# Deformable convolution: hats of three taps in one VectorE instruction, and a second group of values copied by VectorE

## The chip, the core and the metric

The kernel runs on one core of a Trainium2 chip. The metric is the device time of one execution in microseconds (us), the median of several runs. A core has four engines that compute, each with its own instruction queue, worked off in order: TensorE (PE in the profile, with PEld for its weight loads), VectorE (DVE), ScalarE (ACT) and GpSimd (POOL). SyncE (SP) issues most DMAs. Engines wait for each other by semaphores.

## The reference, cut to what matters

The input is two images of 64 channels, 128 x 128 pixels, fp32. A small encoder and decoder of 3x3 convolutions is added to it, then a deformable 3x3 convolution is added to that. The change lies in the second:

```python
x = x + _L0_conv_ref(_gn(x), ...)             # encoder, decoder: not touched
x = x + _L1_conv_ref(_gn(x), w_off, b_off, w_def)

offsets = _conv2d(x, w_off, b_off, 1, 1)      # dy, dx for each of 9 taps and each pixel
py = hs + iy + dy                             # where tap k reads, a fraction of a pixel
px = ws + ix + dx
val = gather(y0, x0, (1 - wy) * (1 - wx)) + ...   # bilinear, four neighbours
out = einsum('bckhw,ock->bohw', val, w_def)
```

## The kernel before

Up to about 755 us the kernel computes the first part and the offsets. From there to the end (1282.5 us) it computes the deformable convolution in 32 strips of four output rows, both images at once. A bilinear gather is written as a matrix product: for a window of pixels and a tap, the weight of a pixel is hat(y distance) x hat(x distance), with hat(d) = 1 - min(|d|, 1). For each strip and each of the nine taps (UNITS = 9):

- TensorE makes the distances of a tap in one of two PSUM slots (`distances`, L1039, eight matmuls).
- ScalarE takes their absolute value into the SBUF tile `dist` (`absolute`, L1460, 128x1024: both images, and y and x side by side). `dist` holds six taps (DIST_RING).
- VectorE clamps it in place, min(d, 1) - 1 (`hats`, L1850, 128x1024), and multiplies the y half by the x half into the tile `hat` (`product`, L1860, 128x512). `hat` is double, one half for each of two strips.

When the nine taps of a strip are in `hat`, TensorE multiplies windows of pixels by them in six groups (`sample_group`, L1086): groups 0 to 3 of three blocks, groups 4 and 5 of two, with a few narrow matmuls of the edges behind group 5 (L1098). Even groups use PSUM banks 4 and 5, odd ones banks 6 and 7. A group's values are copied to the SBUF tile `val`: group 2 by VectorE (L511), the others by ScalarE (L1463), where group 5 has two small edge copies behind it. Then TensorE multiplies `val` by the weights in four parts (`weigh`, L1160 and L1155, banks 6 and 7), and VectorE adds the residual (`strip_result`, L1886, output `outt`).

The order on each engine is written out by hand. In step s TensorE runs, for n = 0 to 8, `distances(s + 1, n)`, then the parts of `weigh(s - 1)` at n = 1, 2, 3 and 4, then the groups of strip s: group 0 at n = 5, groups 1 and 2 at n = 6, group 3 at n = 7, groups 4 and 5 at n = 8. So one step of TensorE reads

d0 d1 W01 d2 W23 d3 W45 d4 W678 d5 G0 d6 G1 G2 d7 G3 d8 G4 G5 edges

with d the distances of the next strip, W the weighing of the last one by taps and G the groups of this one. These short names are used below. W01 waits until all six groups of the last strip are copied. G1 waits for the result of the last strip (its banks hold the sum), G2 and later ones for the copy of the group two ahead, and dn for the absolute value of tap n - 2. ScalarE runs the absolute value of tap n, then the copies of the groups of that n. VectorE runs, for each n, the hats of tap n and the product of tap n - 1; the result of the last strip stands ahead of the hats at n = 5 (RESULT_AT), and the copy of group 2 behind the product at n = 6.

Of the kernel before, what the change touches and what calls it, by code (L numbers as in the profile page):

```python
# [10 lines left out]
ALU = mybir.AluOpType  # L11
# [69 lines left out]
DIST_RING = 6  # L81
# [4 lines left out]
ACT_GROUPS = [0, 1, 3, 4, 5]  # L86
DVE_GROUPS = [2]
# [3 lines left out]
RESULT_AT = 5  # L91
# [81 lines left out]
def build(nc, x, w4, w3, wds, wdec, woff, boff, wdef, wtaps, gmat, ident, sel, rampc, selg, places, out):  # L173
    es = ExitStack()
    with es:
# [103 lines left out]
        dist = in_stage("dist", [P, DIST_RING, 2, BANK])  # L279
# [241 lines left out]
        def dist_at(j, n):  # L521

            return dist[:, (UNITS * j + n) % DIST_RING]

# [278 lines left out]
        def _(pe):  # L803
# [252 lines left out]
            def sample_group(s, j, count, g):  # L1056

                if g == 0:
                    pe.wait_ge(win_in[j], count)
                    pe.wait_ge(prod_dve, UNITS * (s + 1))  # L1060
                    settled(pe)
# [186 lines left out]
        def _(act):  # L1248
# [200 lines left out]
            def absolute(s, j, n, first=False):  # L1449
                act.wait_ge(dist_made, UNITS * s + (n + 1))  # L1450

                if n >= DIST_RING or not first:
                    m_ = n - DIST_RING
                    q = s if m_ >= 0 else s - 1
                    m_ %= UNITS
                    act.wait_ge(prod_dve, UNITS * q + (m_ + 1))
                elif n == DIST_RING - 1:
                    act.wait_ge(edge_hats, 1)
                slot = 2 * dist_slot(j, n)
                act.activation(dist_at(j, n), psum[:, slot:slot + 2, :], ACT.Abs).then_inc(dist_abs, 1)  # L1460
# [47 lines left out]
            def edge_absolute(e):  # L1508
                act.wait_ge(edge_dist, e + 1)
                if e:  # L1510
                    act.wait_ge(prod_dve, UNITS * STRIPS)
                act.activation(dist[:, DIST_RING - 1, :, 0:K * W0], psum[:, 0:2, 0:K * W0], ACT.Abs).then_inc(edge_abs, 1)

# [26 lines left out]
        def _(dve):  # L1540
# [305 lines left out]
            def hats(s, j, n):  # L1846

                dve.wait_ge(dist_abs, UNITS * s + (n + 1))
                d = dist_at(j, n)
                dve.tensor_scalar(d, d, 1.0, 1.0, ALU.min, ALU.subtract).then_inc(hats_made, 1)  # L1850

            def product(s, j, n):
                if n == 0 and not (isinstance(s, int) and s < 2):
                    dve.wait_ge(vals_made, GROUPS * (s - 1))
                    settled(dve)
                dve.wait_ge(hats_made, UNITS * s + (n + 1))
                d = dist_at(j, n)
                lo = TAP_PITCH * n + n % K
                to = hat[:, j, lo:lo + BANK].rearrange("p (b n) -> p b n", b=IMAGES)
                dve.tensor_tensor(to, d[:, :, 0:PS * HALF_W], d[:, :, PS * HALF_W:], ALU.mult).then_inc(prod_dve, 1)  # L1860

            def edge_product(e):
                d = dist[:, DIST_RING - 1, :, 0:K * W0]
# [25 lines left out]
            def strip_step(s, j, uses, last=False):  # L1889

                for n in range(UNITS):
                    if n == RESULT_AT and not (isinstance(s, int) and s == 0):
                        strip_result(s - 1, 1 - j, uses if j else uses - 1)
                    if not last:
                        hats(s + 1, 1 - j, n)
                        if n > 0:
                            product(s + 1, 1 - j, n - 1)
                    elif n == 0:
                        edge_product(1)
                    for g in GROUPS_AT.get(n, []):  # L1900
                        if g in DVE_GROUPS:
                            take_group(s, j, g)
                if not last:
                    product(s + 1, 1 - j, UNITS - 1)
# [11 lines left out]
            for n in range(UNITS):  # L1916
                hats(0, 0, n)
                product(0, 0, n)
# [229 lines left out]
```

## Time and profile before

| | us |
|---|---|
| median of 3 runs | 1282.44 (1280.95 to 1284.28) |
| the profiled execution, its span | 1282.5 |
| strips, first result to last but two (29 steps) | 795.83 to 1235.28 |
| absolute values (L1460), busy, of 288 | 288.8 |
| hats (L1850), busy, of 288 | 202.3 |
| products (L1860), busy, of 288 | 195.3 |
| copies of group 2 (L511), busy, of 32 | 33.7 |

Of the profiled execution the page gives the span alone as its time; it lies 0.1 us from the median. Busy times add up instructions, which overlap by a tenth of a microsecond where one starts before the last has ended. TensorE's clock is given as a share of 2.4 GHz: 1.00 and 0.50 are its two levels here.

### The profile page before, as it was taken

Reading aid. Unit: us, or ns where it says so; the run is one execution under the profiler, and the core shown is the slowest. Engines: PE = TensorE matmul, PEld = TensorE weight load, DVE = VectorE, ACT = ScalarE, POOL = GpSimd, SP = SyncE. Lnnn points to the kernel's source line nnn. Section 1 sums busy time; section 2 is a strip of 40 time slices with the busy share of each in tenths; the row PEclk is TensorE's granted clock in tenths of the full one; section 3 lists DMA queues with packets and bytes.
Section 4 is the critical chain, followed back from the end, with each engine's and each line's share of the span. In section 5 each row is a group of like instructions: output and inputs, shape, how many; then the busy total and the mean of one; then the engine's idle time right before and its main releaser. Section 6 shows DMA issues by size and latency. Waiting matters only on the chain.

```text
span 1282.5 us, 41555 instructions
## 1 busy us (share of the span) xinstructions
PE 1055.9 (82%) x16938; PEld 669.3 (52%) x16938; DVE 888.9 (69%) x1378; ACT 672.1 (52%) x907; POOL 62.4 (5%) x89
## 2 busy tenths in 40 slices
PE   0799999987595999999974957888778887888784
PEld 0234446664242455446642426666666766666664
DVE  5877762334988878742528948888878887888870
ACT  0532433112166333331113477888788887988771
POOL 0000000000052000000000440000000000000000
PEclk9999999999797999999998978999999998999997
DMA  8000023150643000211305254443434443444421
GB/s 200 1 1 2 2 96 67 40 128 1 165 106 85 1 1 1 96 34 35 68 1 150 78 135 129 137 135 114 127 111 124 122 132 105 131 130 117 114 81 34
DMA packets 78797, 107.02 MB, mean 83 GB/s; under 512 B 10511, under 2 KB 67047, under 8 KB 75928
## 3 DMA queue, kind: packets, MB, share of 16 engines
q1 hardware_dynamic: 78472, 103.18, 29.9%
q8 instruction: 144, 2.36, 0.8%
q10 hardware_dynamic: 144, 1.18, 0.3%
q14 instruction: 37, 0.30, 0.1%
HBM read 74.85 MB, written 29.47 MB: 81 GB/s over the span
## 4 chain that ended last, share of the span: by engine, by line
issue 45%; PE 38%; DVE 9%; ACT 2%; POOL 2%; DMA 1%; SPq 0%; POOLq 0%; DVEq 0%; ACTq 0%
PE psum L843 23%; PE psum L912 13%; DVE tp L1749 2%; DVE v L1637 2%; DMA x_odd<-x 1%; PE psum L953 1%; DVE stats L1817 1%; POOL offp L2022 1%; POOL offr L2018 1%; ACT xm L1383 1%; PE psum L934 1%; DVE xm L1804 1%; DVE tm L1755 1%; PE psum L943 1%; DVE xm L1688 1%
## 5 line engine op out<-in xcount | busy, mean ns | idle before, releaser
L843 PE MATMUL psum<-v,u 64*64 64x512 f32 x3072 | 337.1, 597 | 19.7 <-DVE v L1637 14.6
L1460 ACT ACTIVATE dist<-psum 128x1024 f32<-128x1024 f32 x288 | 288.8, 1027 | 51.3 <-PE psum L1039 40.1
L843 PEld LDWEIGHTS psum<-v,u 64*64 64x64 f32 x3072 | 148.1, 134 | 207.1 <-issue 190.4
L1850 DVE TENSOR_SCALAR dist<-dist 128x1024 f32<-128x1024 f32 x288 | 202.3, 703 | 73.3 <-ACT dist L1460 71.4
L1086 PE MATMUL psum<-hat,win 64*64 64x144 f32 x4096 | 197.3, 319 | 36.0 <-DVE outt L1886 20.8
L1860 DVE TENSOR_TENSOR hat<-dist 128x512 f32<-128x512 f32 x288 | 195.3, 687 | 0.3
L1160 PE MATMUL psum<-val,wdefs 64*64 64x256 f32 x1944 | 161.2, 392 | 32.1 <-ACT val L1463 23.6
L1086 PEld LDWEIGHTS psum<-hat,win 64*64 64x64 f32 x4096 | 152.3, 136 | 64.2 <-issue 63.3
L1463 ACT ACTIVATE val<-psum 128x864 f32<-128x864 f32 (+3 forms) x230 | 146.8, 677 | 32.6 <-PE psum L1086 24.5
L1039 PE MATMUL psum<-offs,sels 61*64 61x256 bf16 x2304 | 134.7, 283 | 26.2 <-issue 16.3
L1160 PEld LDWEIGHTS psum<-val,wdefs 64*64 64x64 f32 x1944 | 95.4, 137 | 48.4 <-issue 41.2
L1039 PEld LDWEIGHTS psum<-offs,sels 61*64 61x64 bf16 x2304 | 87.8, 111 | 51.9 <-issue 42.0
L1637 DVE TENSOR_TENSOR v<-stage 128x1024 f32<-128x1024 f32 x64 | 75.2, 1221 | 20.5 <-ACT stage L1331 20.5
L976 PE MATMUL psum<-tm,woffs 64*32 64x512 f32 x1152 | 71.0, 633 | 11.4 <-DVE tm L1755 11.4
L1322 ACT ACTIVATE mid<-psum 128x1024 f32<-128x1024 f32 x32 | 32.8, 1024 | 85.4 <-PE psum L843 85.4
L1637 DVE TENSOR_TENSOR v<-xm 128x1024 f32<-128x1024 f32 (+1 forms) x64 | 73.4, 1212 | 5.7 <-ACT xm L1339 4.1
L1339 ACT ACTIVATE xm<-xm 128x2048 f32<-128x2048 f32 x16 | 30.8, 1923 | 81.9 <-DVE xm L1688 81.9
L1678 DVE TENSOR_TENSOR psum<-mid,psum 128x1024 f32<-128x1024 f32 x32 | 39.4, 1230 | 42.1 <-ACT mid L1322 42.1
L1578 DVE SCALAR_TENSOR_TENSOR hxm<-psum,hxm 128x256 f32<-128x256 f32 x32 | 13.6, 424 | 72.6 <-PE psum L912 72.3
L912 PE MATMUL psum<-htm,w3s 64*64 64x256 f32 x1152 | 63.0, 375 | 0.0
L1331 ACT ACTIVATE stage<-psum 128x1024 f32<-128x1024 f32 x32 | 36.3, 1142 | 46.8 <-PE psum L843 46.8
L1155 PE MATMUL psum<-val,wdefs 64*64 64x256 f32 x396 | 57.9, 387 | 0.0
(146 smaller groups left out, 988.5 us busy)
## 6 DMA issues: line engine op xcount, KB each, us to landing
win<-pixd SPq DMA_DIRECT2D x256, 68.0 KB
win<-pixd SPq DMA_DIRECT2D x128, 136.0 KB
raw<-x SPq DMA_DIRECT2D x16, 512.0 KB, 7.8
x1d<-xm SPq DMA_DIRECT2D x16, 512.0 KB, 6.0
pixd<-turned SPq DMA_DIRECT2D x64, 128.0 KB, 2.4
x1t<-x1d SPq DMA_DIRECT2D x63, 128.0 KB, 2.7
out<-outt SPq DMA_DIRECT2D x63, 128.0 KB, 2.8
offs<-offd SPq DMA_DIRECT2D x32, 162.0 KB
```

The lines of the kernel that those rows point to most:

```text
L843: mm = pe.matmul(o, u4[half, i, v, ky, :], V[half, at:at + CHUNK, cg, v, :], start=start, stop=stop, skip_group_check=True)
L912: mm = pe.matmul(by_rows(o, level), w3s[CH * rg:CH * rg + CH, W_AT[layer], tap, :], rows_in(src, level, stride, rg, slot, step, tap), star ...
L976: mm = pe.matmul(by_rows(o, FULL), woffs[CH * rg:CH * rg + CH, tap, :], rows_in(T, FULL, 1, rg, slot, 4 * half + j, tap), start=tap == 0, ...
L1039: mm = pe.matmul(dst, sels[of, 2 * n + axis, :], offs[of, slot, b, lo:lo + PS * HALF_W], start=True, stop=True, skip_group_check=True)
L1086: mm = pe.matmul(dst[:, :, :, q:q + PS], win[half, j, b, block_ + h, :], rows, start=True, stop=True, skip_group_check=True)
L1155: pe.matmul(dst.rearrange("c (r w) -> c r w", w=W0), w, pair, start=False, stop=False, skip_group_check=True)
L1160: mm = pe.matmul(dst.rearrange("c (r w) -> c r w", w=W0), w, val[half, slot, r0:r0 + 2, cols], start=k == 0, stop=k == TAPS - 1, skip_grou ...
L1460: act.activation(dist_at(j, n), psum[:, slot:slot + 2, :], ACT.Abs).then_inc(dist_abs, 1)
L1463: return act.activation(dst, src, ACT.Copy)
L1637: dve.tensor_tensor(dst, a, c, op).then_inc(v_made[v], 1)
L1850: dve.tensor_scalar(d, d, 1.0, 1.0, ALU.min, ALU.subtract).then_inc(hats_made, 1)
L1860: dve.tensor_tensor(to, d[:, :, 0:PS * HALF_W], d[:, :, PS * HALF_W:], ALU.mult).then_inc(prod_dve, 1)
```

## The change

`dist` keeps its size, six taps, but is now two buffers of three taps. ScalarE still takes one tap per instruction, and waits for VectorE only at the first tap of each three. VectorE clamps three taps in one instruction (128x3072) and multiplies three in one (128x1536), so a strip has three hats and three products instead of nine of each. Their order in a step is hats 0, product 0, hats 1, result of the last strip, product 1, copy of group 2, hats 2, product 2, copy of group 4. The copy of group 4 has moved there from ScalarE. TensorE's order is the same; its wait at G0 of the next strip for the copy of group 4 now names VectorE.

```diff
-DIST_RING = 6
+DIST_RING = 2
+TRIPLES = UNITS // K
-ACT_GROUPS = [0, 1, 3, 4, 5]
-DVE_GROUPS = [2]
+ACT_GROUPS = [0, 1, 3, 5]
+DVE_GROUPS = [2, 4]
-RESULT_AT = 5
+RESULT_AT = 1
+DVE_GROUPS_AT = {1: [2], 2: [4]}
...
-        dist = in_stage("dist", [P, DIST_RING, 2, BANK])
+        dist = in_stage("dist", [P, DIST_RING, K, IMAGES, BANK])
...
-            return dist[:, (UNITS * j + n) % DIST_RING]
+            return dist[:, (TRIPLES * j + n // K) % DIST_RING, n % K]
...
-                    pe.wait_ge(prod_dve, UNITS * (s + 1))
+                    pe.wait_ge(prod_dve, TRIPLES * (s + 1))
...
             def absolute(s, j, n, first=False):
                 act.wait_ge(dist_made, UNITS * s + (n + 1))
-                if n >= DIST_RING or not first:
-                    m_ = n - DIST_RING
-                    q = s if m_ >= 0 else s - 1
-                    m_ %= UNITS
-                    act.wait_ge(prod_dve, UNITS * q + (m_ + 1))
-                elif n == DIST_RING - 1:
+                if first and n == K * (DIST_RING - 1):
                     act.wait_ge(edge_hats, 1)
+                elif n % K == 0 and not (first and n < K * DIST_RING):
+                    act.wait_ge(prod_dve, TRIPLES * s + (n // K + 1 - DIST_RING))
...
-            def hats(s, j, n):
-
-                dve.wait_ge(dist_abs, UNITS * s + (n + 1))
-                d = dist_at(j, n)
+            def hats(s, j, i):
+
+                dve.wait_ge(dist_abs, UNITS * s + K * (i + 1))
+                d = dist[:, (TRIPLES * j + i) % DIST_RING]
                 dve.tensor_scalar(d, d, 1.0, 1.0, ALU.min, ALU.subtract).then_inc(hats_made, 1)
 
-            def product(s, j, n):
-                if n == 0 and not (isinstance(s, int) and s < 2):
+            def product(s, j, i):
+
+                if i == 0 and not (isinstance(s, int) and s < 2):
                     dve.wait_ge(vals_made, GROUPS * (s - 1))
                     settled(dve)
-                dve.wait_ge(hats_made, UNITS * s + (n + 1))
-                d = dist_at(j, n)
-                lo = TAP_PITCH * n + n % K
-                to = hat[:, j, lo:lo + BANK].rearrange("p (b n) -> p b n", b=IMAGES)
-                dve.tensor_tensor(to, d[:, :, 0:PS * HALF_W], d[:, :, PS * HALF_W:], ALU.mult).then_inc(prod_dve, 1)
+                dve.wait_ge(hats_made, TRIPLES * s + (i + 1))
+                d = dist[:, (TRIPLES * j + i) % DIST_RING]
+                first = K * TAP_PITCH * i
+                to = hat[:, j, first:first + BANK]
+                to = bass.AP(to.tensor, to.offset, [to.ap[0], [TAP_PITCH + 1, K], [HALF_STRIP, IMAGES], [1, HALF_STRIP]])
+                dve.tensor_tensor(to, d[:, :, :, 0:HALF_STRIP], d[:, :, :, HALF_STRIP:], ALU.mult).then_inc(prod_dve, 1)
...
             def strip_step(s, j, uses, last=False):
 
-                for n in range(UNITS):
-                    if n == RESULT_AT and not (isinstance(s, int) and s == 0):
+                for i in range(TRIPLES):
+                    if not last:
+                        hats(s + 1, 1 - j, i)
+                    elif i == 0:
+                        edge_product(1)
+                    if i == RESULT_AT and not (isinstance(s, int) and s == 0):
                         strip_result(s - 1, 1 - j, uses if j else uses - 1)
                     if not last:
-                        hats(s + 1, 1 - j, n)
-                        if n > 0:
-                            product(s + 1, 1 - j, n - 1)
-                    elif n == 0:
-                        edge_product(1)
-                    for g in GROUPS_AT.get(n, []):
-                        if g in DVE_GROUPS:
-                            take_group(s, j, g)
-                if not last:
-                    product(s + 1, 1 - j, UNITS - 1)
+                        product(s + 1, 1 - j, i)
+                    for g in DVE_GROUPS_AT.get(i, []):
+                        take_group(s, j, g)
```

VectorE's queue in a step, before, in one of the steps outside the loop (`TENSOR_SCALAR` is hats, `TENSOR_TENSOR hat` a product, `dist_abs` ScalarE's absolute values, `strip_conv` the end of W678):

```order
L1850 TENSOR_SCALAR dist<-dist 128x1024 [waits dist_abs]
L1860 TENSOR_TENSOR hat<-dist 128x512 [waits hats_made]
L1886 TENSOR_TENSOR outt<-psum,x1t 128x512 [waits out_done1,x1_in1,strip_conv]
L1850 TENSOR_SCALAR dist<-dist 128x1024 [waits dist_abs]
L1860 TENSOR_TENSOR hat<-dist 128x512 [waits hats_made]
L1850 TENSOR_SCALAR dist<-dist 128x1024 [waits dist_abs]
L1860 TENSOR_TENSOR hat<-dist 128x512 [waits hats_made]
L511 COPY val<-psum 128x2x36x12 [waits strip_conv,vals_made]
L1850 TENSOR_SCALAR dist<-dist 128x1024 [waits dist_abs]
L1860 TENSOR_TENSOR hat<-dist 128x512 [waits hats_made]
L1850 TENSOR_SCALAR dist<-dist 128x1024 [waits dist_abs]
L1860 TENSOR_TENSOR hat<-dist 128x512 [waits hats_made] x2
```

The same step now, whole:

```order
L1849 TENSOR_SCALAR dist<-dist 128x3072 [waits dist_abs]
L1861 TENSOR_TENSOR hat<-dist 128x3x512 [waits vals_made,hats_made]
L1849 TENSOR_SCALAR dist<-dist 128x3072 [waits dist_abs]
L1887 TENSOR_TENSOR outt<-psum,x1t 128x512 [waits out_done1,x1_in1,strip_conv]
L1861 TENSOR_TENSOR hat<-dist 128x3x512 [waits hats_made]
L513 COPY val<-psum 128x2x36x12 [waits strip_conv,vals_made]
L1849 TENSOR_SCALAR dist<-dist 128x3072 [waits dist_abs]
L1861 TENSOR_TENSOR hat<-dist 128x3x512 [waits hats_made]
L513 COPY val<-psum 128x2x36x8 [waits vals_made]
```

The result has moved from behind a product and ahead of the sixth tap's hats to behind a hats instruction that covers the sixth tap, and a copy stands behind the last product.

ScalarE's queue at the end of a step before: the absolute value of tap 8, the copies of groups 4 and 5, the two edge copies.

```order
L1460 ACTIVATE dist<-psum 128x1024 [waits prod_dve,dist_made]
L1470 REGISTER_ALU
L1463 ACTIVATE val<-psum 128x2x36x8 [waits vals_made]
L1470 REGISTER_ALU
L1463 ACTIVATE val<-psum 128x2x36x8 [waits vals_made]
L1463 ACTIVATE val<-psum 128x2x3x4 [waits vals_act]
L1463 ACTIVATE val<-psum 128x2x3x4
```

And now:

```order
L1459 ACTIVATE dist<-psum 128x1024 [waits dist_made]
L1469 REGISTER_ALU
L1462 ACTIVATE val<-psum 128x2x36x8 [waits vals_made]
L1472 ISA
L1462 ACTIVATE val<-psum 128x2x3x4 [waits vals_act]
L1462 ACTIVATE val<-psum 128x2x3x4
```

One of the two copies is gone from ScalarE; the one left is group 5's.

## Rows read from the trace of the kernel before

**Rows 1.** Waits of TensorE (PE), 796 to 1247 us: us total, times, longest

```profile
PE psum L1160 <- ACT val L1463: 23.0, 22, 1.2
PE psum L1086 <- DVE outt L1886: 20.8, 27, 1.2
PE psum L1039 <- issue: 16.3, 15, 3.6
```

**Rows 2.** Window, three clean strips: busy PE, PEld, DVE, ACT, POOL (instructions); clock; DMA

```profile
978.50:1022.50 44.00, 37.40 (x864) 30.64 (x864) 38.38 (x62) 39.02 (x49) 0.00 (x0) 1.00 0.42 122
```

**Rows 3.** Timeline of VectorE: start us, us, engine line op

```profile
795.83 0.68 DVE L1886 TENSOR_TENSOR outt<-psum,x1t 128x512 f32<-128x512 f32 x1
...
993.27 0.69 DVE L1886 TENSOR_TENSOR outt<-psum,x1t 128x512 f32<-128x512 f32 x1
...
1007.14 0.69 DVE L1860 TENSOR_TENSOR hat<-dist 128x512 f32<-128x512 f32 x1
1007.74 0.69 DVE L1886 TENSOR_TENSOR outt<-psum,x1t 128x512 f32<-128x512 f32 x1
...
1235.28 0.68 DVE L1886 TENSOR_TENSOR outt<-psum,x1t 128x512 f32<-128x512 f32 x1
```

**Rows 4.** Timeline of TensorE, one clean strip and the next one's start

```profile
991.33 0.42 PE L1039 MATMUL psum<-offs,sels 61*64 61x256 bf16 x8
...
994.10 2.05 PE L1086 MATMUL psum<-hat,win 64*64 64x144 f32 x48 [0.80 <-DVE outt L1886]
...
997.33 0.46 PE L1039 MATMUL psum<-offs,sels 61*64 61x256 bf16 x8
...
1001.37 1.09 PE L1160 MATMUL psum<-val,wdefs 64*64 64x256 f32 x16 [0.92 <-ACT val L1463]
...
1006.40 0.42 PE L1039 MATMUL psum<-offs,sels 61*64 61x256 bf16 x8
...
1008.58 0.67 PE L1086 MATMUL psum<-hat,win 64*64 64x144 f32 x12 [0.61 <-DVE outt L1886]
```

**Rows 5.** Timeline of ScalarE, the same strip

```profile
998.48 1.02 ACT L1460 ACTIVATE dist<-psum 128x1024 f32<-128x1024 f32 x1
999.38 1.70 ACT L1463 ACTIVATE val<-psum 128x576 f32<-128x576 f32 x4
...
1006.87 1.03 ACT L1460 ACTIVATE dist<-psum 128x1024 f32<-128x1024 f32 x1 [0.49 <-PE psum L1039]
```

**Rows 6.** Instructions of tiles dist and val: duration ns min/median/max

```profile
L1850 DVE TENSOR_SCALAR dist<-dist x288: 682/693/3993, 758.1 to 1241.5; 128x1024 f32<-128x1024 f32 x144
L1860 DVE TENSOR_TENSOR hat<-dist x288: 682/686/698, 762.1 to 1242.8; 128x512 f32<-128x512 f32 x144
...
L1867 DVE TENSOR_SCALAR dist<-dist x2: 560/560/561, 757.0 to 1244.4; 128x768 f32<-128x768 f32 x2
L1871 DVE TENSOR_TENSOR hat_e<-dist x2: 558/558/559, 757.6 to 1245.0; 128x384 f32<-128x384 f32 x2
...
L511 DVE COPY val<-psum x32: 1049/1053/1059, 781.2 to 1250.7; 128x864 f32<-128x864 f32 x32
```

**Rows 7.** Timeline of VectorE ahead of the first strip

```profile
762.75 0.69 DVE L1850 TENSOR_SCALAR dist<-dist 128x1024 f32<-128x1024 f32 x1
763.47 0.69 DVE L1860 TENSOR_TENSOR hat<-dist 128x512 f32<-128x512 f32 x1
```

**Rows 8.** Timeline of TensorE around two falls of its clock

```profile
914.43 0.30 PE L1039 MATMUL psum<-offs,sels 61*64 61x256 bf16 x4 [2.10 <-issue]
...
1076.74 1.07 PE L1039 MATMUL psum<-offs,sels 61*64 61x256 bf16 x16 [3.60 <-issue]
1077.57 1.95 PE L1160 MATMUL psum<-val,wdefs 64*64 64x256 f32 x16
...
1084.29 0.40 PE L1039 MATMUL psum<-offs,sels 61*64 61x256 bf16 x8
```

**Rows 9.** Window behind the first of them (columns as in Rows 2)

```profile
915.00:917.00 2.00, 2.00 (x40) 1.98 (x40) 1.16 (x2) 1.23 (x2) 0.00 (x0) 0.50 0.48 148
```

More of the change, by code:

```diff
@@ L1510, in edge_absolute @@
                 if e:
-                    act.wait_ge(prod_dve, UNITS * STRIPS)
-                act.activation(dist[:, DIST_RING - 1, :, 0:K * W0], psum[:, 0:2, 0:K * W0], ACT.Abs).then_inc(edge_abs, 1)
+                    act.wait_ge(prod_dve, TRIPLES * STRIPS)
+                act.activation(dist[:, DIST_RING - 1, 0, :, 0:K * W0], psum[:, 0:2, 0:K * W0], ACT.Abs).then_inc(edge_abs, 1)
             edge_absolute(0)
@@ L1844, in _ @@
             dve.tensor_scalar(flag[:], psum[0:1, STAT_BANK, 0:1], 0.0, None, ALU.is_gt).then_inc(flag_set, 1)
-            def hats(s, j, n):
-                dve.wait_ge(dist_abs, UNITS * s + (n + 1))
-                d = dist_at(j, n)
+            def hats(s, j, i):
+                dve.wait_ge(dist_abs, UNITS * s + K * (i + 1))
+                d = dist[:, (TRIPLES * j + i) % DIST_RING]
                 dve.tensor_scalar(d, d, 1.0, 1.0, ALU.min, ALU.subtract).then_inc(hats_made, 1)
-            def product(s, j, n):
-                if n == 0 and not (isinstance(s, int) and s < 2):
+            def product(s, j, i):
+                if i == 0 and not (isinstance(s, int) and s < 2):
                     dve.wait_ge(vals_made, GROUPS * (s - 1))
                     settled(dve)
-                dve.wait_ge(hats_made, UNITS * s + (n + 1))
-                d = dist_at(j, n)
-                lo = TAP_PITCH * n + n % K
-                to = hat[:, j, lo:lo + BANK].rearrange("p (b n) -> p b n", b=IMAGES)
-                dve.tensor_tensor(to, d[:, :, 0:PS * HALF_W], d[:, :, PS * HALF_W:], ALU.mult).then_inc(prod_dve, 1)
+                dve.wait_ge(hats_made, TRIPLES * s + (i + 1))
[4 more added lines that the diff above has]
+                dve.tensor_tensor(to, d[:, :, :, 0:HALF_STRIP], d[:, :, :, HALF_STRIP:], ALU.mult).then_inc(prod_dve, 1)
             def edge_product(e):
-                d = dist[:, DIST_RING - 1, :, 0:K * W0]
+                d = dist[:, DIST_RING - 1, 0, :, 0:K * W0]
                 dve.wait_ge(edge_abs, e + 1)
@@ L1915, in _ @@
             edge_product(0)
-            for n in range(UNITS):
-                hats(0, 0, n)
-                product(0, 0, n)
+            for i in range(TRIPLES):
+                hats(0, 0, i)
+                product(0, 0, i)
             strip_step(0, 0, 1)
```

## The prediction

> **What bounds the kernel now.** I read the windows of the strips first: three clean strips take 44.0 us, 14.67 each, at a clock of 1.00, and in them TensorE is busy 37.4, VectorE 38.4 and ScalarE 39.0 us, 85 to 89% each [rows 2]. No engine is full, so the period is set by a chain that goes from engine to engine, and what counts is where the chain runs, not the sum of an engine's work. From the first result at 795.83 to the one at 1235.28 there are 29 steps of 15.15 us on average [rows 3]; the 0.48 us above 14.67 comes with a few stretches in which TensorE waits for nothing shown ("issue") or its clock falls [rows 1, 8].
>
> TensorE's waits then name the links of the chain [rows 1]. Two recur nearly each strip: W01 waits for ScalarE's copies (23.0 us in 22 strips) and G1 for VectorE's result (20.8 us in 27). All else that waits is the third line and smaller. So there are two links to price: A, from the end of d8 to the start of W01, and B, from the end of d5 to the start of G1. Between them TensorE mostly works without a wait: W01 to the end of d5 is 1001.37 to 1006.82, 5.45 us, and G1 to the end of d8 is 994.10 to 997.79, 3.69 us [rows 4].
>
> Link A now: d8 ends at 997.79, W01 starts at 1001.37: 3.58 us [rows 4]. In it ScalarE finishes tap 8's absolute value at 999.50, 1.71 behind d8, and the copies of groups 4 and 5 with their edges at 1001.08 [rows 5]. Link B now: 1006.82 to 1008.58, 1.76 us, and one strip earlier 991.75 to 994.10, 2.35 us; mean 2.05 [rows 4].
>
> **Prices of the new instructions.** No row has a hats of 3072 or a product of 1536 elements. Hats take 0.693 us at 1024 and 0.560 at 768, 0.52 ns for an element; products 0.686 at 512 and 0.558 at 384, 1.00 ns [rows 6]. Drawn out, a three-tap hats is 0.693 + 2048 x 0.00052 = 1.76 us, a product 0.686 + 1.024 = 1.71. The other end is three of today's at their 0.60 us step [rows 3]: 1.80. The copy of group 4 (576 elements) on VectorE is 1.053 - 0.288 = 0.77 by the same 1.00 ns, and not above the 1.05 of 864 [rows 6]. An instruction that needs nothing of the last starts 0.09 before its end (0.60 against 0.69), one that waits for it 0.03 behind (762.75, 0.69 long, then 763.47) [rows 3, 7].
>
> VectorE's own work changes by little: 18 steps of 0.60 (10.8) become 3 x (1.76 + 1.71) + small gaps, about 10.3, and the copy puts 0.7 back. ScalarE loses 0.65 us a strip. Neither is the bound, so this is priced at nothing by itself.
>
> **Removed from link A.** The copy of group 4 leaves ScalarE. But the copy of group 5 waits for G5 and its edge matmuls, and ScalarE came to it at about 1000.0, when these ended; so ScalarE would be done at most about 0.1 us sooner. The relief is near nothing.
>
> **Added to link A.** VectorE's last three instructions of a step are now hats of taps 6, 7 and 8, their product, and the copy of group 4, in this order. The hats wait for tap 8's absolute value, which waits for d8. W01 waits for the copy. Behind the end of d8: absolute value done at 1.71; hats 1.74 to 3.50; product 3.53 to 5.24; copy 5.15 to 5.92; W01 at 6.06, with the 0.14 that G1 at 994.10 takes behind the result's end at 993.27 + 0.69 [rows 3, 4]. That is 6.06 against 3.58: **+2.5 us**. Group 4's values are ready long before; its copy just stands behind 3.5 us of work for the next strip. W01 cannot be passed on TensorE's queue, and d0 and d1 of the next strip are done by then. Ends: with instructions at 1.80 and a copy of 1.05, +3.0; if the larger ones gain more than drawn out (1.6 each, the bare 3072 x 0.52 and 1536 x 1.04 ns), +2.2.
>
> **Added to link B.** The result now stands behind hats of taps 3, 4 and 5, which wait for tap 5's absolute value and so for d5. Before, it stood ahead of that tap's hats and W678, which ends before d5, released it. Behind the end of d5: absolute value done at 1.08 (1006.82 to 1007.90) [rows 4, 5]; hats 1.11 to 2.87; result 2.78 to 3.47; G1 at 3.61. Against the mean 2.05: **+1.55 us**. Ends: +1.3 and +1.9, by which of the two strips is taken [rows 4]. Behind G1 wait G2, d7, G3 and d8, so it all reaches link A.
>
> The chain closes: W01, d5, result, G1, d8, copy, W01, 5.45 + 3.6 + 3.7 + 6.05 = 18.8 us, with each part held by the last. Nothing can run ahead: VectorE's hats 0 end long before d5, product 2 of a strip is needed by TensorE only a step later, and the windows' DMAs have 4 us more. The six-tap buffer costs nothing: ScalarE's tap 3 of the next strip needs product 2, done before W01 starts.
>
> Link A is paid 31 times (W01 of strips 0 to 30; the last strip has no hats to wait for), link B 30 times: 31 x 2.5 + 30 x 1.55 = 77.5 + 46.5 = 124 us. Ahead of the first strip the long hats and products move the start by under 2 us either way, and the last strip's second VectorE copy is free. So far 1282.5 + 124 = **1406**.
>
> **What the longer gaps do to the clock.** TensorE's wait ahead of W01 grows from 0.92 [rows 4] to 3.4 us, the one ahead of G1 from 0.6 to 0.8 to about 2.2. Behind an idle of 2.10 us the clock was 0.50 [rows 8, 9], and behind 3.60 us the same work from W01 to the end of d5 took 1077.57 to 1084.69, 7.12 us in place of 5.45: +1.67 [rows 4, 8]. So I expect the clock to fall to 1.2 GHz in most strips ahead of W01, and now and then ahead of G1. What it costs a strip lies between 0 and 1.67 + 1.0 (G1 and G2, 2.05 us at 1.00, half as long again); I take 1.5, near the row of 3.60, as the idle of 3.4 is nearest to it: 30 x 1.5 = +45. Against this, stalls of the "issue" kind that fall ahead of W01, as the 3.60 us one did, vanish in the wait that is there anyway: of 16.3 us [rows 1] half, -8; ends 0 and -16. Sum: 1406 + 45 - 8 = **1443 us**. The profiled execution's span is within 0.1 us of the median of the runs, so this stands for the median too.
>
> **A rule weighed.** A product that waits for the hats just ahead starts 0.72 us behind their start, and an independent one 0.60 [rows 3, 7]. The Trainium skill (VectorE: DVE Perf Modes, The DRAIN you can't avoid) says that a semaphore between chained VectorE instructions costs nothing extra, since the pipeline empties anyway. By it, link A would be 0.12 us shorter, 4 us in all; the rows decide for the longer.
>
> **Rivals.** (1) *The clock holds at 1.00.* For it: TensorE still works about 12.5 of 18.8 us a strip. Against it: the clock fell behind idle times of 2.10 and 3.60 us [rows 8, 9]. It gives 1406 - 8 = 1398. (2) *Both gaps bring the clock down each strip*: 30 x 2.67 = 80, so 1406 + 80 = 1486. (3) *Only link A is real*: if TensorE is held elsewhere between d5 and G1, or the result slips ahead, B vanishes: 1443 - 46 = 1397, with the clock. (4) *The other side, faster.* G1 waits for the end of VectorE's queue ahead of the result. Were that queue limited by its own work, and not by tap 5, fewer instructions would empty it sooner: 12 fixed costs of about 0.08 us (1.80 - 1.72) less, and the 20.8 us of waits for the result go, with some of those for ScalarE: about 1260. It decides if tap 5's absolute value is ready more than 1.7 us before W678 ends; today it is ready 1.3 us after (W678 ends at about 1006.6). The Trainium skill (same page, The TRN2 errata) gives this reading support: an instruction's fixed latency is paid once by a large tile and again by each small one. The trace agrees on the size of the instructions, not on where they stand. (5) *The edit does not do what it says*: ScalarE is relieved but gains nothing, since group 5 waits for its matmuls; that is in the sum.
>
> **How the numbers follow.** Forecast with partial clock loss 0.60 (1415 to 1475 by its own ends); clock holds 0.17 (1398); both gaps 0.10 (1486); only A 0.08 (1397); faster 0.03 (1260); all hidden, within 0.3% (about what a measurement of this kernel can tell from no change), 0.02. The range takes in rivals 1 to 3 down to 1392 and up to 1490: within it the first four mostly fall, and it leaves out both other signs and the tails. Faster 0.03, same 0.02, slower 0.95.
>
> **What would show it.** In the profile after: results about 19 to 21 us apart; L1849 near 1.76 and L1861 near 1.71 us; TensorE's longest waits ahead of W01 on VectorE's copy (L513), over 3 us each, and ahead of G1 on the result (L1887), about 2 us; the strips' clock under 0.95; ScalarE idle for PE more than before. It would be wrong if W01 waited for ScalarE still, if results came under 17 us apart, or if the clock stayed at 1.00.

## The result, and the profile after

| kernel | median, us | runs | ratio to before, 95% interval |
|---|---|---|---|
| before | 1281.7 | 1280.43 to 1284.28 | |
| changed | 1486.76 | 1485.28 to 1487.24 | 1.1587 (1.1557 to 1.1616) |

The change costs 205 us, 16%. The profiled execution has a span of 1485.2 us, 202.7 more than that of before. Two kernels below had one execution each that took far longer (5828 and 2174 us, against 1338 and 1279); no ratio and no profile shown here is from them. The page gives the busy time of each engine, and of the hats the line, engine, operation and tiles, count, busy us and mean ns, idle time ahead and what ended most of it.

```profile
PE 1135.3 (76%) x16938; PEld 725.6 (49%) x16938; DVE 887.0 (60%) x1026; ACT 656.1 (44%) x875; POOL 62.5 (4%) x89
...
L1849 DVE TENSOR_SCALAR dist<-dist 128x3072 f32<-128x3072 f32 x96 | 171.8, 1790 | 231.6 <-ACT dist L1459 231.6
```

VectorE is 887.0 us busy, where the page of before has 888.9: twelve instructions a strip fewer, one copy more. But it waits 231.6 us for ScalarE's absolute values ahead of its hats, where it waited 71.4. What that costs TensorE its waits tell (800 to 1437 us; us in total, times, longest; they answer to [rows 1]):

```profile
PE psum L1162 <- DVE val L513: 106.1, 27, 4.1
PE psum L1088 <- DVE outt L1887: 74.0, 30, 2.5
PE psum L1041 <- issue: 8.9, 2, 4.5
```

W01 now waits for VectorE's copy of group 4, 3.9 us a strip, and no more for ScalarE. G1 waits for the same result as before, 2.5 us in place of 0.8. These are the two links of the forecast. Here they are on TensorE, in the columns of [rows 4]:

```profile
1052.76 1.99 PE L1162 MATMUL psum<-val,wdefs 64*64 64x256 f32 x16 [3.94 <-DVE val L513]
...
1058.99 0.41 PE L1041 MATMUL psum<-offs,sels 61*64 61x256 bf16 x8
...
1063.01 3.16 PE L1088 MATMUL psum<-hat,win 64*64 64x144 f32 x48 [2.46 <-DVE outt L1887]
...
1067.29 0.41 PE L1041 MATMUL psum<-offs,sels 61*64 61x256 bf16 x8
...
1074.05 1.98 PE L1162 MATMUL psum<-val,wdefs 64*64 64x256 f32 x16 [3.91 <-DVE val L513]
```

and on VectorE, the same strip ([rows 3]):

```profile
1051.61 0.75 DVE L513 COPY val<-psum 128x576 f32<-128x576 f32 x1
...
1060.50 1.76 DVE L1849 TENSOR_SCALAR dist<-dist 128x3072 f32<-128x3072 f32 x1 [0.68 <-ACT dist L1459]
1062.18 0.68 DVE L1887 TENSOR_TENSOR outt<-psum,x1t 128x512 f32<-128x512 f32 x1
...
1069.43 1.76 DVE L1849 TENSOR_SCALAR dist<-dist 128x3072 f32<-128x3072 f32 x1 [2.15 <-ACT dist L1459]
1071.23 1.76 DVE L1861 TENSOR_TENSOR hat<-dist 128x1536 f32<-128x1536 f32 x1
1072.90 0.75 DVE L513 COPY val<-psum 128x576 f32<-128x576 f32 x1
```

The result (L1887) starts when hats 1 ends; G1 starts at 1063.01, 3.60 us behind the end of d5 at 1059.41. d8 ends at 1067.70; then come tap 8's absolute value, hats 2 at 1069.43, product 2 at 1071.23 and the copy at 1072.90, which ends at 1073.65; the next W01 started at 1074.05, 6.35 us behind d8. Results lie 21.06 to 22.9 us apart, in 29 steps from 802.29 to 1430.82, mean 21.67, against 15.15.

The clock is the other half of it. Windows (us; busy TensorE matmuls, weight loads, VectorE, ScalarE, GpSimd with instructions; granted clock; DMA; GB/s) at the two places, and over four and a half strips:

```profile
1050.00:1052.00 2.00, 0.00 (x0) 0.00 (x0) 2.00 (x2) 1.30 (x2) 0.00 (x0) 1.00 0.61 182
1052.00:1054.00 2.00, 1.24 (x12) 0.88 (x16) 0.36 (x1) 0.00 (x0) 0.00 (x0) 0.68 0.71 218
1064.00:1066.00 2.00, 2.00 (x41) 1.97 (x39) 0.53 (x1) 0.96 (x1) 0.00 (x0) 0.50 0.57 132
```

```profile
900.00:1000.00 100.00, 70.81 (x1332) 58.52 (x1336) 58.71 (x41) 57.01 (x67) 0.00 (x0) 0.81 0.30 84
```

After both idle times of this strip, 3.94 us ahead of W01 and 2.46 ahead of G1, the clock is at its lower level, and it is 0.81 on average over 100 us, where [rows 2] had 1.00. By the time that TensorE's work took, it was so behind both idle times in all 30 strips: W01 to the end of d5 took 6.44 to 7.94 us, G1 to the end of d8 4.58 to 4.76, where they take 5.00 and 3.67 with the clock held (the filled kernel below).

Where the 202.7 us are: 29 steps of 21.67 - 15.15 make 189.1; the first result is 6.5 us later, the time behind result 29 is 54.4 us in place of 47.2, 7.2 more. The steps' 6.52 us divide, by the filling experiments below, into 18.64 - 14.67 = 4.0 for the two links, 3.0 for the clock, less 0.5 for stalls that the kernel before had in its average.

### The profile page after: what moved, and what is told of

It is laid out like the page before. It is cut to its first block, busy times and chain, and to the rows that moved or that the text cites. A ratio compares the mean times of both kernels' runs of the same rounds, so it can differ in the third digit from the quotient of the medians.

```text
span 1485.2 us, 40996 instructions
## 1 busy us (share of the span) xinstructions
PE 1135.3 (76%) x16938; PEld 725.6 (49%) x16938; DVE 887.0 (60%) x1026; ACT 656.1 (44%) x875; POOL 62.5 (4%) x89
## 4 chain that ended last, share of the span: by engine, by line
issue 52%; PE 34%; DVE 7%; POOL 2%; ACT 2%; DMA 1%; SPq 0%; POOLq 0%; DVEq 0%; ACTq 0%
PE psum L845 20%; PE psum L914 11%; DVE tp L1748 2%; DMA x_odd<-x 1%; PE psum L955 1%; DVE v L1636 1%; DVE stats L1816 1%; POOL offp L2020 1%; POOL offr L2016 1%; ACT xm L1385 1%; PE psum L936 1%; DVE xm L1803 1%; DVE tm L1754 1%; PE psum L945 1%; DVE stats L1806 0%
## 5 line engine op out<-in xcount | busy, mean ns | idle before, releaser
L1849 DVE TENSOR_SCALAR dist<-dist 128x3072 f32<-128x3072 f32 x96 | 171.8, 1790 | 231.6 <-ACT dist L1459 231.6
L1162 PE MATMUL psum<-val,wdefs 64*64 64x256 f32 x1944 | 210.2, 493 | 110.3 <-DVE val L513 110.1
L1088 PE MATMUL psum<-hat,win 64*64 64x144 f32 x4096 | 228.1, 362 | 83.6 <-DVE outt L1887 74.0
L1088 PEld LDWEIGHTS psum<-hat,win 64*64 64x64 f32 x4096 | 185.2, 166 | 102.6 <-issue 102.0
L1162 PEld LDWEIGHTS psum<-val,wdefs 64*64 64x64 f32 x1944 | 112.6, 174 | 133.8 <-issue 123.6
L1462 ACT ACTIVATE val<-psum 128x864 f32<-128x864 f32 (+3 forms) x198 | 126.4, 660 | 109.8 <-PE psum L1088 85.4
L1861 DVE TENSOR_TENSOR hat<-dist 128x1536 f32<-128x1536 f32 x96 | 168.6, 1756 | 2.3
L1041 PE MATMUL psum<-offs,sels 61*64 61x256 bf16 x2304 | 144.9, 323 | 19.2 <-ACT dist L1459 9.3
L1041 PEld LDWEIGHTS psum<-offs,sels 61*64 61x64 bf16 x2304 | 96.8, 131 | 52.5 <-issue 41.0
L1636 DVE TENSOR_TENSOR v<-stage 128x1024 f32<-128x1024 f32 x64 | 75.2, 1222 | 20.3 <-ACT stage L1333 20.2
L513 DVE COPY val<-psum 128x864 f32<-128x864 f32 x64 | 57.9, 904 | 46.4 <-PE psum L1088 46.4
L1157 PE MATMUL psum<-val,wdefs 64*64 64x256 f32 x396 | 75.7, 492 | 0.0
```

What stands on the lines that cost most here:

```text
L1041: mm = pe.matmul(dst, sels[of, 2 * n + axis, :], offs[of, slot, b, lo:lo + PS * HALF_W], start=True, stop=True, skip_group_check=True)
L1088: mm = pe.matmul(dst[:, :, :, q:q + PS], win[half, j, b, block_ + h, :], rows, start=True, stop=True, skip_group_check=True)
L1157: pe.matmul(dst.rearrange("c (r w) -> c r w", w=W0), w, pair, start=False, stop=False, skip_group_check=True)
L1162: mm = pe.matmul(dst.rearrange("c (r w) -> c r w", w=W0), w, val[half, slot, r0:r0 + 2, cols], start=k == 0, stop=k == TAPS - 1, skip_grou ...
L1462: return act.activation(dst, src, ACT.Copy)
L1636: dve.tensor_tensor(dst, a, c, op).then_inc(v_made[v], 1)
```

## The experiments

Each is an edit of the changed kernel, if not said otherwise. The forecast's theory is two links of one chain (A: d8 to W01 through the copy of group 4; B: d5 to G1 through the result), each with a fall of the clock behind it. The rival is that the long instructions or the two three-tap buffers themselves hold the strip.

### One link undone at a time, and both

Link B undone (the result ahead of hats 1):

```diff
+                    if i == RESULT_AT and not (isinstance(s, int) and s == 0):
+                        strip_result(s - 1, 1 - j, uses if j else uses - 1)
                     if not last:
                         hats(s + 1, 1 - j, i)
                     elif i == 0:
                         edge_product(1)
-                    if i == RESULT_AT and not (isinstance(s, int) and s == 0):
-                        strip_result(s - 1, 1 - j, uses if j else uses - 1)
```

> The changed kernel with the result of the last strip put ahead of hats 1 on VectorE's queue; the copy of group 4 stays behind product 2. Theory (two links of one chain, each with its fall of the clock): link B, 3.60 us from the end of d5 to G1, falls to about 1.3, and G1 and G2 run at 2.4 GHz: 2.3 + 1.0 us in each of 30 strips, 99 us less, about 1388 us; the wait ahead of W01 stays near 4 us. Rival (the long instructions or the two three-tap buffers hold the strip, wherever the result stands): less than 20 us less, above 1465 us.

Measured: 1396.42 us, ratio 1.0877 (1.084 to 1.0914): 90 us less than the changed kernel, 8 above the expectation. TensorE's waits, 800 to 1360 us:

```profile
PE psum L1162 <- DVE val L513: 100.4, 28, 3.9
PE psum L1088 <- DVE val L513: 17.7, 30, 0.8
...
PE psum L1088 <- DVE outt L1887: 2.8, 6, 0.6
```

The wait for the result is down from 74.0 to 2.8 us; the one ahead of W01 stays. A wait not forecast has come up: G4 waits for the copy of group 2 (17.7 us in 30 strips), which now stands behind product 1 when the groups come earlier. It is about twice the 8 us missing.

Link A undone (the copy of group 4 ahead of hats 2):

```diff
-DVE_GROUPS_AT = {1: [2], 2: [4]}
+DVE_GROUPS_AT = {1: [2, 4]}
```

> The changed kernel with the copy of group 4 put ahead of hats 2 on VectorE's queue, behind that of group 2; the result stays behind hats 1. Theory: link A, 6.1 us from the end of d8 to W01, falls to about 3.3, set by ScalarE's copy of group 5, and W01 to d5 takes 5.45 in place of 6.65: 4.0 us in each of 31 strips, about 1365 us; the wait ahead of G1 stays above 2 us. Rival (long instructions or three-tap buffers): above 1465 us.

Measured: 1338.4 us, ratio 1.0419 (1.0386 to 1.0453): 148 us less, more than the 122 expected. The same kernel again, for its profile:

> The kernel with only the copy of group 4 ahead of hats 2 again, for its profile. Theory: TensorE waits for the result ahead of G1 over 2 us a strip (about 65 us in all), and ahead of W01 no more than before (about 25 us in all, for ScalarE), no wait for VectorE's copy there; strips about 16.7 us apart.

Measured: 1342.09 us. TensorE's waits, 800 to 1420 us:

```profile
PE psum L1088 <- DVE outt L1887: 66.5, 29, 2.5
PE psum L1162 <- ACT val L1462: 21.2, 22, 1.0
PE psum L1041 <- issue: 9.7, 3, 4.7
```

G1's wait is whole, 66.5 us, and W01 waits for ScalarE 21.2 us as before the change, for VectorE no more. Results are 17.00 us apart on average, median 16.71. The surplus over the expectation is the clock's: W01 to the end of d5 takes 5.19 us on average in place of 7.03, 1.8 us less, where the expectation gave 1.2. Behind G1, whose idle time is the same, the clock still fell in most strips, but not in all. Two windows of 2 us from the start of a G1, each behind an idle time of 2.47 or 2.48 us:

```profile
1006.02:1008.02 2.00, 2.00 (x37) 2.00 (x41) 1.52 (x1) 0.41 (x1) 0.00 (x0) 0.58 0.45 128
1038.56:1040.56 2.00, 2.00 (x55) 2.00 (x56) 1.52 (x1) 0.80 (x1) 0.00 (x0) 1.00 0.44 139
```

Of 25 strips with 2.4 to 2.5 us of idle ahead of G1, the first 48 matmuls behind it took the full clock's 2.05 us in four, and more in 21.

Both at once:

> Both edits at once: result ahead of hats 1, copy of group 4 ahead of hats 2, three taps to an instruction as in the changed kernel. Theory: both links are near those of the kernel before, and VectorE has 12 instructions less a strip; a period of 14.1 us at a clock of 1.00 plus about 0.4 for stalls, 1265 to 1290 us, so all of the loss is the place of two instructions. Rival (long instructions or three-tap buffers): above 1400 us.

Measured: 1279.14 us, ratio 0.9964 (0.9944 to 0.9985). The instructions, their number, the buffers and the engine of the copy are those of the changed kernel, 1486.76 us; two instructions stand elsewhere in a queue. So the rival falls: long instructions and three-tap buffers hold nothing by themselves. Undone alone, the links give back 90 and 148 us, 238 in sum; undone together, 208. Some 30 us are in both, so the shares depend on which goes first: B gives 90 first and 59 second (1338 to 1279), A gives 148 first and 117 second (1396 to 1279). No experiment took these 30 us apart. TensorE's waits tell of some 21 of them: with only the result moved, G1 waits 2.8 us for it, and the waits named issue are 10.9 us; with both moved they are 13.9 and 20.5 us, with no long wait ahead of W01 left that could take them up. The wait for the copy of group 2, 17.7 and 18.6 us, is in both kernels that have the result ahead.

### The size of the clock's part

The forecast's least certain term. TensorE was kept at work in the two gaps, with no wait removed: the matmuls of d1 and d6 made again, same operands, same place, before their release.

```diff
+FILL = {1: 7, 6: 4}
...
-                for axis in range(2):
+                for axis in [0, 1] * (1 + FILL.get(n, 0) if not (isinstance(s, int) and s == 0) else 1):
```

> The changed kernel, with TensorE kept at work in the two gaps: the eight matmuls of d1 are made seven more times and those of d6 four more times, with the same operands into the same place, ahead of their release. No wait is taken away and nothing of VectorE or ScalarE changes. Theory (the falls of the clock cost 2.2 to 2.9 us a strip, on top of the links): the clock in the strips is 0.97 or more, a strip takes 18.8 us and the kernel about 1405 us. Rival (the low clock is only a sign of the idle, and costs nothing by itself, or TensorE's work is hidden): 1487 us or more, for the added matmuls.

Measured: 1448.95 us, ratio 1.1294 (1.1262 to 1.1327), neither the one nor the other. The first strips show why. On TensorE:

```profile
830.37 2.13 PE L1042 MATMUL psum<-offs,sels 61*64 61x256 bf16 x71
834.83 1.09 PE L1163 MATMUL psum<-val,wdefs 64*64 64x256 f32 x16 [2.32 <-DVE val L514]
...
839.40 0.43 PE L1042 MATMUL psum<-offs,sels 61*64 61x256 bf16 x8
...
843.45 1.84 PE L1089 MATMUL psum<-hat,win 64*64 64x144 f32 x42 [1.61 <-DVE outt L1888]
```

```profile
805.50:842.60 37.10, 28.56 (x752) 25.02 (x752) 25.57 (x19) 25.54 (x31) 0.00 (x0) 1.00 0.38 103
862.90:1005.00 142.10, 111.71 (x2632) 96.95 (x2632) 89.27 (x64) 89.38 (x106) 0.00 (x0) 0.92 0.33 93
```

The 56 added matmuls of d1 took 1.5 us (71 in 2.13, against 15 in 0.62 without them), so 2.32 and 1.61 us were still idle. In the first two steps the clock held at 1.00, and they are 18.55 us each; from the third on it fell again, 0.92 over the seven behind the third, of 20.3 us each. It fell at the gap ahead of W01 only: behind the gap of 1.6 us ahead of G1, G1 to the end of d8 took 3.66 to 3.68 us in all 30 strips. So the filling was too small. With more, in the same place:

```diff
+FILL = {1: 17, 6: 9}
```

> As the last filling of the gaps, but d1's eight matmuls are made 17 more times and d6's nine more times, since 2.3 us were still idle ahead of W01 and 1.6 ahead of G1 there (eight matmuls took 0.21 us) and the clock fell again in most strips. Theory: no idle of over 1 us is left, the clock in the strips is 0.97 or more, a strip takes 18.55 us as the first three did, 1390 to 1410 us. Rival (added matmuls give back only what the first filling gave, or cost by themselves): 1440 us or more.

Measured: 1450.85 us, ratio 1.132 (1.1288 to 1.1352): by its time, the rival. By its trace, the theory:

```profile
800.00:1200.00 400.00, 359.42 (x9760) 326.61 (x9756) 250.34 (x176) 251.78 (x293) 0.00 (x0) 0.97 0.32 91
```

```profile
PE psum L1042 <- issue: 32.2, 19, 4.4
PE psum L1089 <- DVE outt L1888: 14.7, 29, 0.5
```

The clock is 0.97, the waits ahead of G1 are down to 14.7 us, and nine of 29 steps take 18.63 to 18.75 us. But TensorE now stops 19 times within its own stream, 32.2 us in all, waiting for nothing that the trace shows, with 208 more matmuls a strip. Where it stops inside d1, no idle time is left to take the stop up. So the filling was done with fewer: only the last matmul of each again.

```diff
+FILL = {1: 30, 6: 16}
...
                                            stop=True, skip_group_check=True)
+                if not (isinstance(s, int) and s == 0):
+                    for _ in range(FILL.get(n, 0)):
+                        mm = pe.matmul(dst, sels[of, 2 * n + axis, :], offs[of, slot, b, lo:lo + PS * HALF_W], start=True,
+                                       stop=True, skip_group_check=True)
                 mm.then_inc(dist_made, 1)
```

> The gaps filled with a quarter of the instructions: behind d1 only its last matmul is made 30 times more, behind d6 16 times, one after another (256 columns, about 0.107 us each at 2.4 GHz), 46 added matmuls a strip in place of 208. Theory (the low clock costs 2.6 us or more a strip, and the filling with 208 lost its gain to stalls of TensorE's own instruction stream, 32 us and more of waits named issue): clock in the strips 0.97 or more, most strips 18.6 us apart, 1395 to 1420 us. Rival (added matmuls cost what the clock gives back): 1445 us or more.

Measured: 1426.51 us, ratio 1.1118 (1.109 to 1.1145), 6 us beyond the expected range. Two strips of it, a strip with a stall, and TensorE's waits from 800 to 1420 us:

```profile
1064.90:1102.20 37.30, 33.83 (x669) 30.05 (x668) 25.61 (x20) 25.75 (x30) 0.00 (x0) 1.00 0.32 91
1001.30:1027.60 26.30, 20.95 (x336) 18.09 (x334) 12.85 (x11) 12.93 (x15) 0.00 (x0) 0.81 0.24 66
```

```profile
PE psum L1093 <- DVE outt L1892: 21.9, 30, 0.7
PE psum L1167 <- DVE val L514: 21.4, 28, 4.0
```

W01 and d5 of one strip, d6 with its 16 added matmuls, and G1 and d8 of another:

```profile
1094.36 1.09 PE L1167 MATMUL psum<-val,wdefs 64*64 64x256 f32 x16 [0.66 <-DVE val L514]
...
1098.93 0.43 PE L1042 MATMUL psum<-offs,sels 61*64 61x256 bf16 x8
...
1100.35 1.90 PE L1046 MATMUL psum<-offs,sels 61*64 61x256 bf16 x16
```

```profile
1002.17 2.05 PE L1093 MATMUL psum<-hat,win 64*64 64x144 f32 x48 [0.73 <-DVE outt L1892]
...
1005.36 0.47 PE L1042 MATMUL psum<-offs,sels 61*64 61x256 bf16 x8
```

25 of its 29 steps take 18.54 to 18.69 us, at a clock of 1.00, with all of the changed kernel's instructions and waits in place. **The two links alone make a strip of 18.64 us; the fallen clock adds 3.03.** The chain closes to the hundredth: W01 to the end of d5 5.00 us, link B 3.61, G1 to the end of d8 3.67, link A 6.36, together 18.64. In the changed kernel the same four are 7.03, 3.61, 4.69 and 6.36 (means of 28 strips): the links are the same, and the clock costs 2.03 us behind W01 and 1.02 behind G1. Over 29 steps the filling gave back 29 x (21.67 - 19.22) = 71 us; the first result is 12.6 us later (814.86 against 802.29), since ahead of it the added matmuls have nothing to fill, and the two nearly make up the difference of the spans, 1485.2 - 1426.2 = 59.0. The mean is 19.22 and not 18.64 for two strips in which TensorE stopped for over 4 us and waited for nothing shown (26.2 and 26.4 us, clock 0.81 in the first), and for one of 20.3.

### The two parts of the change alone

The kernel before, with one tap an instruction, and only the copy of group 4 moved to VectorE, behind the hats of tap 8 and product 7:

```diff
-ACT_GROUPS = [0, 1, 3, 4, 5]
-DVE_GROUPS = [2]
+ACT_GROUPS = [0, 1, 3, 5]
+DVE_GROUPS = [2, 4]
```

> The kernel before (one tap an instruction, result ahead of tap 5's hats) with one part of the change: the copy of group 4 on VectorE, behind the hats of tap 8 and the product of tap 7. Theory (only what stands ahead of the copy counts): behind d8 come 1.71 of absolute value, 0.6 of hats, 0.6 of product and 0.77 of copy, so W01 at 3.8 us in place of 3.58, 31 x 0.25 = 8 us more, 1283 to 1295 us. Rival (the copy itself is dearer on VectorE than on ScalarE, or its wait holds the queue): over 1310 us. If ScalarE's relief were worth something: under 1279 us.

Measured: 1296.25 us, ratio 1.0108 (1.0071 to 1.0145), just above the range. VectorE and TensorE in one of its strips:

```profile
1005.91 0.69 DVE L1860 TENSOR_TENSOR hat<-dist 128x512 f32<-128x512 f32 x1
1006.51 0.75 DVE L511 COPY val<-psum 128x576 f32<-128x576 f32 x1
```

```profile
1003.10 0.45 PE L1039 MATMUL psum<-offs,sels 61*64 61x256 bf16 x8
...
1007.65 1.09 PE L1160 MATMUL psum<-val,wdefs 64*64 64x256 f32 x16 [1.67 <-DVE val L511]
```

W01 starts 0.39 us behind the copy's end at 1007.26, where the forecast and this expectation allowed 0.14. So link A is 4.10 us here, 0.5 above before: 31 x 0.5 = 16 us, where 14 were measured. That these agree so well is partly luck, since two more things changed, one against the other: behind the longer wait of 1.7 us ahead of W01 the clock fell in eight strips (W01 to the end of d5 6.4 to 6.7 us in place of 5.0; over the 29 steps it is 0.96, against 0.98 before), and the waits named issue went down from 26.3 us to 8.5. The short form of the mistake costs 1%, the long one, with three taps ahead of the copy, the rest.

Three taps an instruction, the result behind hats 1, but the copy of group 4 on ScalarE as before:

```diff
-ACT_GROUPS = [0, 1, 3, 5]
-DVE_GROUPS = [2, 4]
+ACT_GROUPS = [0, 1, 3, 4, 5]
+DVE_GROUPS = [2]
-DVE_GROUPS_AT = {1: [2], 2: [4]}
+DVE_GROUPS_AT = {1: [2]}
```

> The changed kernel with the copy of group 4 back on ScalarE; three taps an instruction and the result behind hats 1 stay. Theory (link A is only the copy's place): as with the copy ahead of hats 2, which took 1338 us, 1335 to 1352 us, since group 5's copy waits for its matmuls anyway. Rival (moving the copy to VectorE relieves ScalarE): over 1360 us, against 1338 with the copy on VectorE.

Measured: 1347.71 us, ratio 1.0524 (1.0499 to 1.055), within the range. Against 1338.4 and 1342.09 with the copy on VectorE and well placed, ScalarE's relief is worth 6 to 9 us, where the forecast had nothing.

### A version that beats both

The wait for the copy of group 2, met in the kernels with the result ahead (18.6 us where both links are undone), was taken away too: its copy ahead of product 1. The whole edit of the changed kernel:

```diff
                 for i in range(TRIPLES):
+                    if i == RESULT_AT and not (isinstance(s, int) and s == 0):
+                        strip_result(s - 1, 1 - j, uses if j else uses - 1)
                     if not last:
                         hats(s + 1, 1 - j, i)
                     elif i == 0:
                         edge_product(1)
-                    if i == RESULT_AT and not (isinstance(s, int) and s == 0):
-                        strip_result(s - 1, 1 - j, uses if j else uses - 1)
+                    if i == 1:
+                        take_group(s, j, 2)
                     if not last:
                         product(s + 1, 1 - j, i)
-                    for g in DVE_GROUPS_AT.get(i, []):
-                        take_group(s, j, g)
+                    if i == 1:
+                        take_group(s, j, 4)
```

> Result ahead of hats 1, copy of group 4 ahead of hats 2 (1279 us), and now the copy of group 2 ahead of product 1. Theory: TensorE's wait for the copy of group 2 ahead of group 4, 18.6 us in 28 strips there, goes; most of it is passed on, 1262 to 1272 us. Rival (product 1, now behind a wait for G2, holds ScalarE's tap 0 of the next strip and the hats 2 behind it): no change, 1276 to 1285 us.

Measured: **1269.85 us, ratio 0.9908 (0.9891 to 0.9925)**, within the expectation and 0.9% faster than the kernel before. TensorE's waits, 800 to 1240 us:

```profile
PE psum L1162 <- ACT val L1462: 19.1, 21, 1.0
PE psum L1088 <- ACT val L1462: 13.9, 37, 0.7
PE psum L1088 <- DVE outt L1887: 12.7, 21, 0.8
```

No wait for a copy of VectorE is left; results are 14.59 us apart on average, 13.83 at best (before: 15.15 and 14.43). The same order with the copy of group 4 on ScalarE asks what that half of the change is worth when it is placed well:

> The best order so far (result ahead of hats 1, copy of group 2 ahead of product 1: 1270 us with the copy of group 4 on VectorE ahead of hats 2), with the copy of group 4 back on ScalarE. If relieving ScalarE is worth what the two kernels with one link undone differ by (1348 with ScalarE's copy, 1338 to 1342 with VectorE's): 6 to 9 us slower than 1270, 1276 to 1280 us. If the relief is nothing, as forecast for group 5's copy: 1267 to 1273 us.

Measured: 1278.95 us, ratio 0.9978 (0.9962 to 0.9993). So in this order the move of the copy gives 9 us of the 12 gained, and three taps an instruction with the placements the other 3. TensorE's waits, 800 to 1240 us:

```profile
PE psum L1162 <- ACT val L1462: 24.2, 22, 1.3
PE psum L1088 <- ACT val L1462: 16.7, 47, 0.4
PE psum L1041 <- issue: 14.2, 10, 3.5
...
PE psum L1088 <- DVE outt L1887: 6.1, 11, 0.8
```

W01 waits 24.2 us for ScalarE there, 19.1 with the copy on VectorE, the groups 16.7 in place of 13.9: 8 us together. These do not explain the 9 us by themselves, since two other waits changed as much: G1 waits 6.1 us for the result in place of 12.7, and the waits named issue are 26.7 us in all in place of 19.7.

## Why the prediction was right, and where its sizes were off

The direction, the two places and the range held: 1486.76 us lies in 1392 to 1490. The likeliest case, 1443, was 44 us short; the second rival, both gaps bringing the clock down each strip, gave 1486, and that case came true. The case is right, that it is right to 1 us is luck: it had 80 us for the clock, nothing for absorbed stalls and nothing for the two ends. Measured are 88 us for the clock (29 x 3.03), some 12 less for stalls, and 7 us more at the ends than the links account for.

- **New instructions.** Hats 1.76 us (forecast 1.76), product 1.76 (1.71), copy of group 4 0.75 (0.77). Drawn out from two sizes of one shape, they were right to 0.05.

```profile
L1849 DVE TENSOR_SCALAR dist<-dist x96: 1752/1760/4617, 756.8 to 1438.1; 128x3072 f32<-128x3072 f32 x96
L1861 DVE TENSOR_TENSOR hat<-dist x96: 1748/1758/1761, 761.4 to 1439.9; 128x1536 f32<-128x1536 f32 x96
```

- **Link B.** 3.60 us from d5 to G1, forecast 3.61. Its parts lie as they were worked out.
- **Link A.** 6.35 us, forecast 6.06. What was sized wrong is the 0.14 us from the copy to W01, taken from the result and G1; this edge takes 0.40. The rows of before had it [rows 4, 5]: W01 at 1001.37, 0.29 behind ScalarE's last copy at 1001.08. Some 8 us of 31 strips.
- **The period with the clock held.** 18.64 us in the filled kernel, forecast 18.8 by the chain and 14.67 + 4.05 by the differences. That the chain came so near is partly luck: link A was 0.3 us too short in it, and W01 to the end of d5 0.45 too long. Its 5.45 us came from one strip, in which TensorE stopped inside d4 (its second half starts at 1005.00, with 0.25 us of idle named issue). With the clock at 1.00 and no stop it takes 5.00, in the kernel before (from 972.14) as in the filled one.
- **The clock.** The term that was sized wrong, and most of the 44 us: it was taken at 1.5 us a strip, as if the clock fell mostly ahead of W01 only. It fell behind both gaps in every strip, and cost 3.03. In the strip shown, W01 to the end of d5 took 6.65 us and G1 to the end of d8 4.69, against 5.00 and 3.67: +1.65 and +1.0; in the next, the first of them took 7.91 (1074.05 to 1081.96), +2.9. The upper end, 1.67 + 1.0, was too low, since 1.67 is 7.12 less the same 5.45: against 5.00 it would have been 2.12.
- **Absorbed stalls.** The forecast halved the 16.3 us of [rows 1], but all of TensorE's waits named issue come to 26.3 us there. In the changed kernel 8.9 us are left, two stalls of 4.4 and 4.5 us ahead of W01, and since W01 has to wait anyway, they lengthen link A by 0.9 us each only. The strips of before had 0.48 us each on average above the clean ones, 14 us in 29, for stalls and falls of the clock. So this term was nearer 12 us than 8.
- **ScalarE's relief** was priced at nothing, and is worth 6 to 9 us where nothing hides it. Group 5's copy does wait for its matmuls, but with the copy on VectorE W01 waits 5 us less for ScalarE, and the groups 3 us less (the last two kernels). Why W01's wait shrinks by 5 us was not settled, and there the result's wait and the stalls changed as much.
- **The start.** The first result is 6.5 us later. Link A and link B are in it once each, 4.05 us by the forecast; the rest, 2.4, is a little more than the 2 us that the forecast allowed, and most of it is the clock again: the edge matmuls ahead of the first W01 took 5.92 us at 0.50 (786.50 to 792.42), before 3.90 at 1.00 (784.33 to 788.23).
- **The faster rival** was wrong for this order of the queue. With the due instructions first, the kernel is 12 us faster than before, not the 22 that it gave (1260), and only 3 of them come with fewer instructions and the placements, 9 with the copy's move. What decides is what the forecast named, that tap 5's absolute value comes after W678: in the strip shown W678 ended at 1059.18, and the hats of that tap could start at 1060.50 only.
- **Only link A**: falls, since each link undone alone gave back 90 and 148 us.

Of the signs listed, all came but one: results 21 to 23 us apart in place of 19 to 21.

## What to carry to other kernels

Before an instruction is made longer or put behind others, ask of each one behind it who waits for it, and of each one ahead what it itself waits for: two short instructions that TensorE waits for stood behind 1.7 and 3.5 us of work for the next strip, which waits for data that come late. Put what is due now first, and group the work for later behind it: the change that cost 16% gains 0.9% in the better order, though 0.7 of it comes with the copy's move and only some 0.2 with the grouping. Where a forecast lengthens TensorE's idle time, price the lower clock at every gap that is longer than those which the trace shows at full clock, and take what it costs from strips without a stop of their own.

## What the runs showed of the hardware

- In the changed kernel, gaps of 2.46 us ahead of G1 and of 3.9 ahead of W01 were followed by a clock of 0.50 each time (30 and 28 times). Gaps of about 0.7 us (the filled kernel) and of 0.92 (before, [rows 4]) left it at 1.00. In between, the length of the gap alone did not settle it: 2.4 to 2.5 us ahead of G1 alone (link A undone) brought it down in 21 of 25 strips, 2.3 to 2.5 ahead of W01 (the first filling) in 21 of 25, 1.4 to 1.85 ahead of W01 (one tap an instruction, copy on VectorE) in 9 of 27. A gap of 1.6 ahead of G1 brought it down in none of 30 strips in the first filling, but gaps of 1.54 and 1.61 there, with link A undone, both did.
- Single matmuls of 61x64 weights, one after another in the gaps, kept the clock at 1.00.
- Eight bf16 matmuls of 256 columns on four quarters of the array, repeated, take 0.21 us (56 in 1.5 us). On one quarter alone, one after another, 16 took 1.90 us from the first's start to the last's end, about 0.11 each; by this estimate eight would take four times as long.
- TensorE's waits named issue rose from 8.9 us to 32.2 inside its distances, and 3.2 ahead of W01, with 208 more matmuls a strip, and were 8.5 us with 46 more. It was not tested what causes them.
- From the end of VectorE's instruction to the start of TensorE's that waits for it, 0.14 to 0.15 us passed at G1 and 0.39 to 0.40 at W01. At W01 TensorE waits for several semaphores one after another; that this is the reason was not tested.
